# A graph network's edge stage: one tile of source rows in every fourth group fetched row by row from the SyncE and ScalarE queues

## The reference

```
h = relu(layernorm(x));  x = x + gcn(relu(gcn(h, W1, b1)), W2, b2)      # first part: two graph convolutions
h = relu(layernorm(x))                                                  # second part
w   = silu(edge_attr @ We1 + be1) @ We2 + be2                           # per edge, 200000 x 128
m   = w * (h[src] @ Wlin)                                               # the source node's row times w
agg = segment_sum(m, dst)
out = x + h + silu(agg @ Wn1 + bn1) @ Wn2 + bn2
```

## Time and profile before

| | |
|---|---|
| median of 3 runs | 3518.19 us (3516.44 to 3519.39) |
| the profiled execution's own time | 3519.03 us |
| its span in the profile | 3517.3 us |
| busy, share of the span | PE 84%, DVE 59%, POOL 42%, ACT 27% |
| granted TensorE clock, mean | 0.88 of full speed |
| edge stage, first gather to last gather | 1521 to 3477 us |

### The profile page before, as it was taken

How to read it: one execution, slowest core, us unless ns; L and a number is a source line. 1 busy time by engine, 2 the same in 40 slices (tenths; PEclk the granted TensorE clock), 3 DMA queues, 4 the chain that set the end, 5 groups by cost and what they waited for, 6 DMA issues and landing times.

```text
span 3517.3 us, 70075 instructions
## 1 busy us (share of the span) xinstructions
PE 2970.2 (84%) x19882; PEld 2165.5 (62%) x19883; DVE 2086.3 (59%) x4759; ACT 959.0 (27%) x2055; POOL 1494.5 (42%) x1601
## 2 busy tenths in 40 slices
PE   6979999999999969978877777778778778777777
PEld 4742456777777769955555555555555555555555
DVE  7999999999999844444443344433444334443333
ACT  5110234455666511122222222122122222122221
POOL 0000000000000000057777777777777777777774
PEclk8989999999999989978788888887788888888888
DMA  2000011222222269833333333333333333333332
GB/s 62 0 0 1 38 56 74 93 93 107 111 111 110 108 267 346 323 79 80 76 80 79 79 77 79 80 79 78 78 80 79 79 79 79 77 79 80 77 76 67
DMA packets 278864, 324.81 MB, mean 92 GB/s; under 512 B 231024, under 2 KB 238345, under 8 KB 266143
## 3 DMA queue, kind: packets, MB, share of 16 engines
q1 hardware_dynamic: 227518, 217.13, 18.6%
q0 software_dynamic: 51168, 106.07, 11.8%
HBM read 238.00 MB, written 85.09 MB: 92 GB/s over the span
## 4 chain that ended last, share of the span: by engine, by line
POOL 41%; PE 35%; issue 17%; DVE 5%; DVEq 1%; POOLq 1%; ACT 0%; DMA 0%; SPq 0%; ACTq 0%
POOL shared L497 41%; PE pb L1294 9%; PE pa L1294 9%; PE pc L1288 6%; PE pd L1288 5%; PE pd L1252 3%; PE pf L1254 1%; PE pb L1379 1%; DVE shared L952 1%; DVE loop L952 1%; PE pb L1506 0%; PE pa L1372 0%; DVEq L952 0%; PE pb L1262 0%; DVE loop L957 0%
## 5 line engine op out<-in xcount | busy, mean ns | idle before, releaser
L497 POOL DMA_INDIRECT shared<-lin_table,idx x1568 | 1479.6, 944 | 479.0 <-issue 477.5
L1115 DVE TENSOR_TENSOR shared<-pb,shared 128x512 f32<-128x512 f32 x392 | 252.4, 686 | 1171.8 <-DMA shared<-lin_table,idx 1171.8
L526 POOL DMA_DIRECT2D lin_table<-c x12 | 9.2, 770 | 1498.9 <-issue 1308.6
L1453 PE MATMUL pb<-we_sb,shared 128*128 128x128 f32 x3136 | 619.8, 359 | 0.0
L1453 PEld LDWEIGHTS pb<-we_sb,shared 128*128 128x128 f32 x3136 | 526.3, 254 | 119.6 <-issue 119.1
L729 ACT ACTIVATE shared<-pa,be_col 128x512 f32<-128x512 f32 x392 | 247.9, 683 | 1101.7 <-PE pa L1442 1101.7
L1449 PE MATMUL pb<-be_parts,ones 3*128 3x512 bf16 x392 | 177.9, 454 | 404.9 <-DVE shared L1115 404.5
L952 DVE TENSOR_SCALAR shared<-col_h,shared 128x784 bf16<-128x784 f16 x1092 | 402.7, 416 | 5.0 <-issue 4.5
L1449 PEld LDWEIGHTS pb<-be_parts,ones 3*128 3x128 bf16 x392 | 36.5, 93 | 467.8 <-issue 451.0
L1442 PE MATMUL pa<-shared,we_sb 64*128 64x512 f32 x784 | 306.8, 870 | 0.7 <-ACT shared L724 0.7
L1294 PE MATMUL pb<-shared,c 128*128 128x392 bf16 x1568 | 304.0, 329 | 1.6 <-DVE shared L952 0.9
(11 more groups left out here) (233 smaller groups left out, 3813.5 us busy)
## 6 DMA issues: line engine op xcount, KB each, us to landing
adjacency<-shared SPq DMA_DIRECT2D x49, 1568.0 KB, 5.6
shared<-adjacency SPq DMA_DIRECT2D x49, 1568.0 KB, 8.4
shared<-in_edge_attr_dram SPq DMA_DIRECT2D x195, 256.0 KB, 3.0
shared<-lin_table,idx POOLq DMA_INDIRECT x1568
lin_table<-c POOLq DMA_DIRECT2D x12, 256.0 KB, 6.9
out_dram<-xr SPq DMA_DIRECT2D x12, 256.0 KB
shared<-in_dst_dram SPq DMA_DIRECT2D x1, 512.0 KB
shared<-in_src_dram SPq DMA_DIRECT2D x1, 512.0 KB
```

What stands on the lines that cost most here:

```text
L497: pool.indirect_dma_start(out=dest(s, j), out_offset=None, in_=table, in_offset=bass.IndirectOffsetOnAxis(ap=idx[:, s, j:j + 1], axis=0)). ...
L1115: dve.tensor_tensor(msgs[s % 2][:, h, :, :], pb[:, h, :].rearrange("p (i f) -> p i f", f=F), rows[:, h, :, :], ALU.mult).then_inc(msg_read ...
L1453: last = pe.matmul(pb[:, h, i * F:(i + 1) * F], act_t[:, h, i * P:(i + 1) * P], we2_sb[:, :], start=False, stop=(i == 3))
```

## The change

In turns 1 to 47, the eighth tile of the fourth group (`ASIDE = 7`) is no longer gathered by POOL. Its 128 rows of `lin_table` are fetched one by one with ordinary DMAs of one row into one of two side buffers (`aside`, in memory that `table_sb` no longer needs): 72 of them by SP and 56 by ACT, in four portions of 18 and 14, one portion per group of a turn (`fetch_rows`). The row numbers are loaded once, as two lists in one partition, and each portion begins with a register load of its numbers; each DMA takes its source address from a register. SP fetches for the turn at hand behind its edge-feature load; ACT fetches for the next turn behind the index copy. DVE's second multiply in such a group is split in two, one for the three gathered tiles of that half and one for the tile set aside, and DVE first waits for both queues' rows. Besides, of the last group only the three tiles that hold edges are gathered (`LAST_TILES = 3`); what lies in the buffers of its other tiles is multiplied by one-hot columns that are zero for these targets.

```diff
+ASIDE = U - 1
+PICKS = ITERS - 2
+SP_ROWS = 72
+ACT_ROWS = P - SP_ROWS
+LAST_TILES = -(-TAIL // P)
...
+        def fetch_rows(eng, regs, table, k, par, chunk, first, here, rows_in):
+
+            eng.load(regs, table[:, bass.ds(k - 1, 1), chunk * here:(chunk + 1) * here].rearrange("a k r -> a (k r)"))
+            for n in range(here):
+                row = first + chunk * here + n
+                eng.dma_start(aside[par][row:row + 1, :],
+                              lin_table[bass.ds(eng.snap(regs[n], min_val=0, max_val=NB * P - 1), 1), :]).then_inc(rows_in[par], 16)
...
+            def load_turn(it, par=None):
                 for s in range(RING):
                     sp.wait_ge(ea_turned, it * RING + (s - RING + 1))
                     load_ea(it * RING + s, s)
+                    if par is not None:
+                        fetch_rows(sp, row_at, sp_list, it - 1, par, s, 0, SP_ROWS // RING, sp_rows_in)
+            load_turn(1)
+            with sp.Fori(0, PICKS // 2) as i:
+                load_turn(i * 2 + 2, 1)
+                load_turn(i * 2 + 3, 0)
...
-            edge_pass(lin, lin_table, lambda s, j: gat[:, s, j, :], msg_ready, 2)
...
+                    gather(lin, lin_table, linear_rows, s, tiles if s == RING - 1 else U)
...
+            with pool.Fori(1, ITERS - 1) as it:
+                gather_turn(it, ASIDE)
+            gather_turn(ITERS - 1, LAST_TILES)
...
-            with act.Fori(0, ITERS - 1) as it:
+            def act_turn(it, par=None):
                 for s in range(RING):
                     edge_act(it * RING + (s + 1))
-                    after_gather(lin, it, s)
+                    after_gather(lin, it, s, 1 if s == RING - 1 else 0)
+                    if par is not None:
+                        fetch_rows(act, row_at, act_list, it + 1, par, s, SP_ROWS, ACT_ROWS // RING, act_rows_in)
+            act_turn(0, 1)
+            with act.Fori(0, PICKS // 2) as i:
+                act_turn(i * 2 + 1, 0)
+                act_turn(i * 2 + 2, 1)
+            act_turn(PICKS)
...
+                if par is not None:
+                    dve.wait_ge(sp_rows_in[par], before_it * (16 * SP_ROWS) + 16 * SP_ROWS)
+                    dve.sem_inc(passed, 1)
+                    dve.wait_ge(act_rows_in[par], before_it * (16 * ACT_ROWS) + 16 * ACT_ROWS)
+                    dve.sem_inc(passed, 1)
```

More of the change, by code:

```diff
@@ L54 @@
 assert N_NODES <= PAD_DST
+assert SP_ROWS % RING == 0 and ACT_ROWS % RING == 0 and PICKS % 2 == 1
 def gnn_kernel(nc, x, src, dst, edge_attr, W1, b1, W2, b2, We1, be1, We2, be2, Wlin, Wn1, bn1, Wn2, bn2, out):
@@ L179, in gnn_kernel @@
         gat_b = gat_w.bitcast(bf16).rearrange("p (s c) -> p s c", s=RING)
+        table_w = table_sb[:, :, :].rearrange("p b c -> p (b c)").bitcast(fp32)
+        aside = [table_w[:, i * F:(i + 1) * F] for i in range(2)]
+        sp_list = part(table_w, 2 * F, PICKS * SP_ROWS, int32)[0:1, :].rearrange("a (k r) -> a k r", r=SP_ROWS)
+        act_list = part(tmsg_f, 0, PICKS * ACT_ROWS, int32)[0:1, :].rearrange("a (k r) -> a k r", r=ACT_ROWS)
         ea = part(shared2, RING * U * F, RING * U * RBF).rearrange("p (s c) -> p s c", s=RING)
@@ L320, in gnn_kernel @@
         next_hot = sem("next_hot")
+        lists_in = sem("lists_in")
+        sp_rows_in = [sem(f"sp_rows_in{i}") for i in range(2)]
+        act_rows_in = [sem(f"act_rows_in{i}") for i in range(2)]
         base_in = sem("base_in")
@@ L444, in _ @@
                 load_ea(s, s)
-            with sp.Fori(1, ITERS - 1) as it:
+            sp.wait_ge(ln2.stored, 16 * (BATCHES + 1))
+            of_picks = src[RING * GE:(PICKS + 1) * RING * GE].rearrange("(a k e) -> a k e", a=1, e=RING * GE)
+            picked = ((RING - 1) * U + ASIDE) * P
+            sp.dma_start(sp_list, of_picks[:, :, picked:picked + SP_ROWS]).then_inc(lists_in, 16)
+            sp.dma_start(act_list, of_picks[:, :, picked + SP_ROWS:picked + P]).then_inc(lists_in, 16)
+            sp.wait_ge(lists_in, 32)
+            row_at = [sp.alloc_register(f"row_at_sp{i}") for i in range(SP_ROWS // RING)]
+            def load_turn(it, par=None):
                 for s in range(RING):
@@ L451, in _ @@
                 sp.wait_ge(ea_turned, g - RING + 1)
+                fetch_rows(sp, row_at, sp_list, PICKS, 1, s, 0, SP_ROWS // RING, sp_rows_in)
                 if g < G - 1:
@@ L493, in _, with gather @@
                                pattern=[[-1, P]], channel_multiplier=1).then_inc(pool_consts, 1)
-            def gather(ps, table, dest, s):
-                for j in range(U):
+            def gather(ps, table, dest, s, tiles=U):
+                for j in range(tiles):
                     pool.indirect_dma_start(
@@ L531, in _, with linear_rows, gather_turn @@
             pool.wait_ge(ln2.stored, 16 * (BATCHES + 1))
-            edge_pass(lin, lin_table, lambda s, j: gat[:, s, j, :], msg_ready, 2)
+            def linear_rows(s, j):
+                return gat[:, s, j, :]
+            def gather_turn(it, tiles):
+                for s in range(RING):
+                    pool.wait_ge(lin.idx_ready, it * RING + (s + 1))
+                    pool.wait_ge(msg_ready, (it * RING + (s - RING + 1)) * 2)
+                    pool.sem_inc(passed, 1)
+                    gather(lin, lin_table, linear_rows, s, tiles if s == RING - 1 else U)
+            for s in range(RING):
+                pool.wait_ge(lin.idx_ready, s + 1)
+                gather(lin, lin_table, linear_rows, s)
+            with pool.Fori(1, ITERS - 1) as it:
+                gather_turn(it, ASIDE)
+            gather_turn(ITERS - 1, LAST_TILES)
         @block.scalar
@@ L608, in first_idx, with after_gather @@
                     next_idx(ps, s, s)
-            def after_gather(ps, it, s):
-                act.wait_ge(ps.gathered[s], (it + 1) * (16 * U))
+            def after_gather(ps, it, s, less=0):
+                act.wait_ge(ps.gathered[s], it * (16 * (U - less)) + 16 * U)
                 next_idx(ps, (it + 1) * RING + s, s)
@@ L732, in _ @@
             edge_act(0)
-            with act.Fori(0, ITERS - 1) as it:
+            act.wait_ge(lists_in, 32)
+            act.wait_ge(ln2.stored, 16 * (BATCHES + 1))
+            row_at = [act.alloc_register(f"row_at_act{i}") for i in range(ACT_ROWS // RING)]
+            def act_turn(it, par=None):
                 for s in range(RING):
                     edge_act(it * RING + (s + 1))
-                    after_gather(lin, it, s)
+                    after_gather(lin, it, s, 1 if s == RING - 1 else 0)
[6 more added lines that the diff above has]
+            act_turn(PICKS)
             for s in range(RING - 1):
@@ L1105, in _, with messages @@
             dve.sem_inc(passed, 1)
-            def messages(g, turns, s):
+            def messages(g, turns, s, par=None, before_it=None, rows_of=U):
                 rows = gat[:, s, :, :].rearrange("p (i h) f -> p h i f", h=2)
-                dve.wait_ge(lin.gathered[s], turns * (16 * U))
+                if s == RING - 1:
+                    dve.wait_ge(lin.gathered[s], (turns - 1) * (16 * ASIDE) + (16 * U if rows_of == U else 16 * (1 + rows_of)))
+                else:
+                    dve.wait_ge(lin.gathered[s], turns * (16 * U))
                 dve.sem_inc(passed, 1)
+                if par is not None:
[3 more added lines that the diff above has]
+                    dve.sem_inc(passed, 1)
                 for h in range(2):
                     dve.wait_ge(w_mm, g * 2 + (h + 1))
+                    if h == 1 and par is not None:
+                        own = RING - 1
+                        dve.tensor_tensor(msgs[s % 2][:, h, 0:own, :], pb[:, h, 0:own * F].rearrange("p (i f) -> p i f", f=F),
+                                          rows[:, h, 0:own, :], ALU.mult)
+                        dve.tensor_tensor(msgs[s % 2][:, h, own, :], pb[:, h, own * F:RING * F], aside[par], ALU.mult)\
+                           .then_inc(msg_ready, 1)
+                        continue
                     dve.tensor_tensor(msgs[s % 2][:, h, :, :], pb[:, h, :].rearrange("p (i f) -> p i f", f=F),
@@ L1154, in _, with message_turn @@
             one_hots(0, 0)
-            with dve.Fori(0, ITERS - 1) as it:
+            def message_turn(it, par=None, before_it=None):
                 for s in range(1, RING + 1):
@@ L1158, in _ @@
                     group_span(dve, span, g - 1)
-                    messages(g, it + (s // RING + 1), s % RING)
+                    if s == RING - 1:
+                        messages(g, it + 1, s, par, before_it)
+                    else:
+                        messages(g, it + (s // RING + 1), s % RING)
                     one_hots(g, s)
                     group_sums(g - 1, s - 1)
+            message_turn(0)
+            with dve.Fori(0, PICKS // 2) as i:
+                message_turn(i * 2 + 1, 1, i)
+                message_turn(i * 2 + 2, 0, i)
+            message_turn(PICKS, 1, PICKS // 2)
             for s in range(1, RING):
```

(2 more changed lines are left out.)

## The result

Median 3786.91 us (3785.58 to 3788.75, 4 runs) against 3517.35 us before (3516.44 to 3519.39, 4 runs, timed together): a ratio of 1.0766, 95% interval 1.0747 to 1.0785. The change costs 269.6 us; 195 were predicted. The profiled execution took 3786.36 us with a span of 3784.7 (before: 3519.0, with a span of 3517.3).

A forecast was written before the change was run, and what follows sets the result against it. POOL's gather queue was taken as the bound before, at 9.99 us a group. With ACT's ring at 11.1 us, 188 groups add 209 us and the last groups give back 14: 3519 + 209 - 14 = 3714 us, range 3450 to 3800.

The forecast's parts named there:

- ACT's ring: ACT's cycle per group: silus, idx copy, 14 rows, edge-feature copy, PE's layer 1, next silus; 10.6 to 11.6 us, middle 11.1.
- The row's price: Issue time of one single-row DMA on ACT or SP, address arithmetic and gaps included: 0.44 us, at most 0.63.
- the branch that the forecast gave 3526 to 3630 us: Case of a row costing between 0.37 and 0.43 us to issue: time 3526 to 3630 us, chance 0.09.
- The 0.24 us row: Single-partition DMA in the trace before, taken as nearest in size; its 0.24 us went into the 0.44 us per row.
- Rival 1: Issues on ACT are cheap, below about 0.32 us a row; POOL stays the bound, 3454 us; chance 0.28, whole or part.
- Rival 2: ACT issues dearer than SP: 0.50 us a row near 3880 us, 0.63 near 4220; above 3810, 0.10 with Rival 3.
- Rival 3: One DMA engine bounds, from 0.21 us a packet: time as before or more; within the 0.10 for above 3810.
- SP's 9.8 us a group: hidden: SP's queue per group, register load, 18 rows and edge-feature load: 9.8 us, costed at nothing while ACT's ring takes 11.1.
- the groups without rows at the two ends: Seven or so last groups, where PE's about 8 us a group sets the pace, not 9.99: gives back 14 us.
- What was costed at nothing: SP's 9.8 us a group, list loads and table wait, DVE's split multiply and semaphore steps, POOL's idx-copy wait: no time added.
- The rule that spoke for cheap issues: Trainium skill's about 50 ns sequencer dispatch per DMA, most fixed cost in completion; by it a row costs little, Rival 1 wins.

## Why the prediction came out as it did

**Direction, place and range: right.** POOL's queue bound the kernel and lost its place; gathers cost 1.25 us each and 52 of them 65 us (66.7 measured in the kernel without rows). The time, 3787 us, lies in the range, near its top, 73 us above the forecast: 24 of them are ACT's ring (3738 us alone), 49 are SP's queue on top of it.

**The ring on ACT: right as a mechanism, and its size by errors that cancel.** Alone it gives 3738 us and 11.36 us a group, where the forecast had 3714 and 11.1. That the two agree so well is luck:

- Too much: the 14 rows were put at 6.2 us and take 5.4, so 0.8; the silus and the index copy's arithmetic were put at 1.36 us ahead of the rest, but the register load starts 0.38 us behind the start of the silus in the group shown, and 0.68 in the next, so 0.7 to 1.0.
- Too little: the register load was put at 1.03 us and is 1.39 or 3.25, 2.3 on the mean, so 1.3; the loop's edge, 0.3 us a group, was left out, as were 0.1 us before the copy and 0.1 us of layer 1's wait (292.8 / 158 = 1.85 us).

The row's price of 0.38 us lies in the branch that the forecast gave 3526 to 3630 us and a chance of 0.09. The kernel with aligned lists, at 3587 us, is in that branch. What carried the change from there to 3787 is the long register load, which no branch has. (The 0.24 us row from which the price was drawn carried 1280 bytes, not 512: its size was not that of a row.)

**The rivals.** Rival 1 needed a row below 0.32 us to come true in full, and POOL left the chain. Rival 2 needed 0.5 us a row. Rival 3 needed 0.21 us a packet on one crowded DMA engine. The page of after has ACT's rows in a queue of their own:

```profile
q10 hardware_dynamic: 5264, 1.36, 0.2%
```

3785 x 16 x 0.002 / 5264 is about 0.02 us a packet, and the kernel of 16 and 16 rows with ACT's rows moved, which sends as many row DMAs, loses nothing to any.

**"SP's 9.8 us a group: hidden": the step that failed.** The prediction saw the mechanism ("SP at 9.8 would be next") and missed the size. What a group of SP's takes, beside the terms it was given:

| term | predicted us | measured us |
|---|---|---|
| edge load with arithmetic and gaps | 0.58 | 0.55 |
| register load | 1.19 | 2.71 (mean of 1.57 and 3.84) |
| arithmetic and gaps around it | 0.14 | 0.17 |
| 18 rows | 7.9 | 7.42 |
| from the last row to the next edge load | 0 | 0.41 (mean of 0.21 and 0.61) |
| edge of the loop, 2.4 us in 8 groups | 0 | 0.3 |
| group | 9.8 | 11.56 |

From one edge load to that eight groups later the timeline has 2397.11 to 2489.54, 11.55 us a group. At 11.55 SP lies above ACT's 11.36, so SP and not ACT is the chain. Of the 1.76 us that were missing 1.52 are the register load. It was drawn as a line through two loads, 0.53 us for 2 registers and 1.10 for 16, and read off at 14 and 18 without asking where the 14 and the 18 begin. Rows 10 could not show it, since each has one length only; so the load of 14 or 18 was a price to bound from both sides, and it was taken as known.

**The sum, redone with what was measured.** The load row of the whole trace of after begins at 1554.2 and ends at 3711.7 us for 188 portions, 2157.5 / 187 = 11.54 us. 188 x (11.54 - 9.99) = 291 us, where 209 were predicted; the difference to the 270 measured, 21 us, is left for the groups without rows at the two ends, where 14 were predicted.

**What was costed at nothing and was nothing:** the two list loads, DVE's extra multiply and semaphore steps. The kernel with 16 and 16 rows and ACT's rows moved has them all and runs at the time of the one without rows. POOL's wait for the idx copy grew to 141 us in the trace of after, but POOL was not on the chain.

**The rule that spoke for cheap issues.** ACT's row DMA occupies the issuing queue for 0.214 us and SP's for 0.228, of steps of 0.38 to 0.42. The Trainium skill (DMA: Bandwidth & Descriptors, Anatomy of one DMA), in a section on DMAs that GpSimd issues, puts the sequencer's dispatch at about 50 ns. For these DMAs, which SP and ACT issue, the traces show four times that; the price came out near the one drawn from the 0.24 us row.

## What to carry to other kernels

Work moved to an idle queue is paid where that queue stands in a dependence ring, not by its idle share: ask for whom the instruction behind it is waited for, and put the moved work right after the last thing others wait for (here 3619 us became 3451). Cost every queue that receives work against the pace you want to reach (9.7 us a group here), not against another new bound that you expect to cover it. And lay out lists that registers are loaded from so that each portion begins at a multiple of 16 bytes.

## What the runs showed of the hardware

**A register load's time depends on where it starts.** Aligned, 16 registers took 1.15 us on SP and 1.20 on ACT, 14 took 1.40, 18 took 1.57; the same 14 and 18 starting 8 bytes off took 3.2 and 3.8 us, about 0.13 us more for each register. Even when aligned, 14 take longer than 16; no run shows why. The Trainium skill (DMA: Bandwidth & Descriptors, Latency and other measured facts) gives a floor of about 600 ns for such a load; the 2-register load of 0.53 us lies a little below it, all the others far above.

**A long loop body pays at its edge.** SP's step back to the loop's head, and the next instruction on its queue (2390 to 2600 us):

```profile
L482 SPq COMPARE_BRANCH  x2: 53/53/53, 2476.8 to 2569.2; - x2
L482 SPq FUSED_REGOPS  x2: 68/68/68, 2479.2 to 2571.9; - x2
```

From the branch to the next instruction are 2.4 us, every eight groups; the body holds 144 rows of three instructions each. The kernel without rows has the same loop with eight edge-feature loads and no rows in its body, and there the next instruction follows in about 0.1 us (2390 to 2600 us):

```profile
L482 SPq COMPARE_BRANCH  x3: 45/45/45, 2393.2 to 2548.6; - x3
L482 SPq FUSED_REGOPS  x3: 68/68/68, 2393.3 to 2548.8; - x3
```

So the length of the body decides, not the branch. The page's queue of code had 159 packets and 1.29 MB before and 162 in the kernel without rows; it has 277 with one engine's rows and 391 with both:

```profile
q14 instruction: 391, 3.20, 0.3%
```

Each engine with rows adds 114 or 115 packets, 5 for each of the 23 passes of its loop. The Trainium skill (Runtime: NRT & Kernel Launch, Instruction fetch mechanics) says that a taken branch to code outside the window held on chip has to fetch it first. The traces agree: the pause and the packets both come with the long body.

**A single row's DMA costs its issuer more than half of what a load of 256 KB does.** One row of 512 bytes takes 0.228 us on SP and 0.214 on ACT, where the load of 1024 pieces takes 0.37 to 0.40. Fetching one tile of 128 rows in this way spends 128 x 0.4 = 51 us of queues to save one gather of 1.25, which pays only while those queues have nothing else to do.
